# Routing softmax moved behind the FFN's router, FFN weights split once and loaded as halves

## The reference, cut to what matters

```python
# FFN (second stage): 1376 hidden columns, padded to 11 chunks of 128
scores = sigmoid(x @ W_router)                    # 8 low-rank experts, top 2
gate = x @ W_gate + lora(x, sA_gate, sB_gate) + expert_lora(x, A_gate, B_gate, w)
up   = x @ W_up   + lora(x, sA_up, sB_up)     + expert_lora(x, A_up, B_up, w)
hidden = silu(gate) * up
out = hidden @ W_down + lora(hidden, ...) + expert_lora(hidden, ...)

# mixture (fourth stage): routing over 64 experts
scores = softmax(xf @ router_w.T)
topk_w, topk_idx = top_k(scores, 8)
topk_w = topk_w / (topk_w.sum(-1) + 1e-20)
pos = (cumsum(onehot) * onehot).sum(-1) - 1       # place of a token in its expert's list
```

## Time and profile before

| | |
|---|---|
| median of 3 runs | 1468.19 us (1467.01 to 1469.37) |
| the profiled execution's own time | 1467.43 us |
| its span, first to last instruction | 1465.6 us |
| mean granted TensorE clock | 0.925 |
| PE busy | 1249.2 us, 85% |
| VectorE, ScalarE, GpSimd busy | 750.8, 508.1, 521.9 us |
| moved by DMA | 181.07 MB |

### The profile page before, as it was taken

How to read it: one execution, slowest core, us unless ns; L and a number is a source line. 1 busy time by engine, 2 the same in 40 slices (tenths; PEclk the granted TensorE clock), 3 DMA queues, 4 the chain that set the end, 5 groups by cost and what they waited for, 6 DMA issues and landing times. The chain is left out here.

```text
span 1465.6 us, 19315 instructions
## 1 busy us (share of the span) xinstructions
PE 1249.2 (85%) x6516; PEld 911.3 (62%) x6516; DVE 750.8 (51%) x1441; ACT 508.1 (35%) x1145; POOL 521.9 (36%) x539
## 2 busy tenths in 40 slices
PE   0698999887899988789998778999637999999990
PEld 0566777655777765577776557777435666666660
DVE  7674645576666667666666766452571222222220
ACT  1582322565232156523215652221122323333330
POOL 3530323633033373302337330132104455555551
PEclk9998999997989999888999988899857999999995
DMA  7002221000322100032210002541415999999966
GB/s 256 1 1 89 79 105 53 0 1 30 121 92 92 53 1 1 30 121 98 85 53 1 2 30 85 204 172 67 194 61 168 334 333 343 358 353 351 292 103 129
DMA packets 45600, 181.07 MB, mean 124 GB/s; under 512 B 6412, under 2 KB 9484, under 8 KB 36692
## 3 DMA queue, kind: packets, MB, share of 16 engines
q1 hardware_dynamic: 30660, 140.23, 25.5%
q0 software_dynamic: 14864, 39.85, 12.0%
HBM read 149.36 MB, written 34.90 MB: 126 GB/s over the span
## 5 line engine op out<-in xcount | busy, mean ns | idle before, releaser
L2024 PE MATMUL PS<-WE,XGT 128*128 128x384 f32 x512 | 195.1, 504 | 1.5 <-DVE HM L1597 0.8
L678 POOL CAST HH<-HID 128x512 fp32r<-128x512 f32 x44 | 38.9, 884 | 366.5 <-DVE HID L1504 366.5
L810 ACT ACTIVATE P<-PS,NM 128x512 f32<-128x512 f32 (+3 forms) x256 | 132.3, 539 | 51.4 <-DVE NM L1217 50.6
L1620 PE MATMUL PS<-XTH,WHI 128*128 128x512 f32 x352 | 144.2, 410 | 0.3 <-ACT SIL L953 0.3
L1621 PE MATMUL PS<-XTL,WHI 128*128 128x512 f32 x352 | 141.0, 401 | 0.0
L1622 PE MATMUL PS<-XTH,WLO 128*128 128x512 f32 x352 | 140.5, 399 | 0.0
L1457 DVE TENSOR_TENSOR WLO<-WRAW,WHI 128x584 fp32r<-128x584 f32 (+1 forms) x88 | 109.7, 1246 | 38.6 <-ACT WHI L939 30.8
L2024 PEld LDWEIGHTS PS<-WE,XGT 128*128 128x128 f32 x512 | 88.2, 192 | 57.9 <-issue 23.5
L1217 DVE TENSOR_REDUCE NM<-PS 128x2 f32<-128x1024 f32 (+2 forms) x96 | 98.6, 1041 | 49.7 <-PE PS L1629 49.2
L1680 PE MATMUL PS<-ident,P 128*128 128x128 f32 x640 | 105.2, 305 | 21.9 <-ACT P L810 12.7
L939 ACT ACTIVATE WHI<-WRAW 128x1280 fp32r<-128x1280 f32 x44 | 56.1, 1274 | 167.4 <-DMA WRAW<-in_ffn 161.6
(11 more groups left out here) (282 smaller groups left out, 2811.3 us busy)
## 6 DMA issues: line engine op xcount, KB each, us to landing
WE<-in_we SPq DMA_DIRECT2D x64, 1152.0 KB, 8.1
WRAW<-in_ffn SPq DMA_DIRECT2D x44, 932.0 KB, 4.6
acc<-HN SPq DMA_DIRECT2D x17, 256.0 KB, 5.1
XIN<-in_x SPq DMA_DIRECT2D x4, 1024.0 KB, 9.4
out<-X SPq DMA_DIRECT2D x4, 1024.0 KB, 4.2
out<-acc POOLq DMA_DIRECT2D x1, 4096.0 KB, 23.3
hx<-HN SPq DMA_DIRECT2D x3, 1152.0 KB, 4.8
CTX<-in_ctx SPq DMA_DIRECT2D x4, 256.0 KB, 6.7
```

The costliest lines, as they stand in the source:

```text
L810: act.activation(prob(t, n), PS[:, c0:c0 + (t + 1) * P], ACT.Exp, bias=NM[:, c:c + 1], accum_out=SSUM[:, c:c + 1]).then_inc(S["p_ready"], 1)
L1620: pe.matmul(dst, a[0], b_[0], start=first, stop=False, **kw)
L2024: mm = pe.matmul(bank(2 + s % 2, 0, 2 * F1), XGT[s % 2][:, k, :], WE[s][:, k * 2 * F1:(k + 1) * 2 * F1], start=(k == 0), stop=(k == KC - 1))
```

## The change

Three things change.

1. The routing softmax of batch b-1 is cut in two. `gates_begin` (row maximum, subtraction) stays ahead of the router's chain; `gates_rest` moves behind chunk 0. With it front_norms of the next batch moves from behind chunk 0 to behind chunk 1, front_scales from chunk 1 to chunk 2, PE's `positions` from chunk 0 to chunk 1, VectorE's from chunk 1 to chunk 3. The one-hot matmuls of the lists come in two pairs (at chunks 4 and 8) in place of single tiles at 2, 4, 6, 8; their first matmul now opens the bank, and the two zeroing matmuls per batch go.
2. The weights are split in batch 0 only. WHI and WLO are replaced by WGU (high and rest of the gate and up piece, 128 x 2560) and WDN (of the down piece, 128 x 1168), two slots each. Batch 0 stores each to a new DRAM tensor `split`, 1280 KB and 584 KB a chunk.
3. Batches 1 to 3 load both back, 1280 KB and 584 KB a chunk, straight into WGU and WDN, with semaphores of their own. The load of WGU waits until gate_up(f-2) is done on PE, that of WDN until down(f-2) is done. WRAW, ScalarE's copies and VectorE's subtractions are not used there.

```diff
-    WHI = [sb(f"WHI{s}", [P, WCOLS], F32R) for s in range(2)]
-    WLO = [sb(f"WLO{s}", [P, WCOLS], F32R) for s in range(2)]
+    WGU = [sb(f"WGU{s}", [P, 2, WD], F32R) for s in range(2)]
+    WDN = [sb(f"WDN{s}", [P, 2, WCOLS - WD], F32R) for s in range(2)]
...
+            def store_gu(f):
+                sp.wait_ge(S["wg_hi"], 1 + f + 1)
+                sp.wait_ge(S["wg_lo"], 1 + f + 1)
+                alone(sp, "sp")
+                sp.dma_start(split[span(f, P), 0:2 * WD], flat(WGU[f % 2])).then_inc(split_stored[f % 2], 16)
...
+                if b == 0:
+                    sp.dma_start(WRAW[0][:, :], w["ffn"][0:P, :]).then_inc(w_loaded[0], 16)
+                    sp.dma_start(WRAW[1][:, :], w["ffn"][P:2 * P, :]).then_inc(w_loaded[1], 16)
+                else:
+                    for slot in range(2):
+                        sp.wait_ge(split_stored[slot], 32 * SLOT_LOADS[slot])
+                    for f in range(2):
+                        load_gu(f)
+                        load_dn(f)
...
                 if b > 0:
                     store_rows(b - 1)
...
+                if b == 0:
+                    store_gu(0)
                 for f in range(2, NF):
-                    load_w(f, f % 2)
+                    if b == 0:
+                        store_gu(f - 1)
+                        down_made(f - 2)
+                        sp.dma_start(WRAW[f % 2][:, :], w["ffn"][span(f, P), :]).then_inc(w_loaded[f % 2], 16)
+                        store_dn(f - 2)
+                    else:
+                        sp.wait_ge(S["up_ps"], 1 + b * NF + f - 1)
+                        alone(sp, "sp")
+                        load_gu(f)
+                        sp.wait_ge(S["dn_ps"], 1 + b * NF + f - 1)
+                        alone(sp, "sp")
+                        load_dn(f)
                     if last and f < 8:
                         load_expert(f - 2, f - 2)
...
+                def wg_hi(f, slot):
+
+                    act.wait_ge(w_loaded[slot], 16 * (f // 2 + 1))
+                    if f > 1:
+                        act.wait_ge(split_stored[slot], 32 * (f // 2))
+                    act.activation(WGU[slot][:, 0, :], WRAW[slot][:, 0:WD], ACT.Copy).then_inc(S["wg_hi"], 1)
...
-                w_rest(0, 0, 0, WD, "wg_hi", "wg_lo")
-                if b > 0:
+                if b == 0:
+                    w_rest(0, WGU, 0, WD, "wg_hi", "wg_lo")
+                else:
                     dve.wait_ge(S["lgt_ps"], 1 + b)
-                    gates(b - 1, bank(1, 0, NT * E1).rearrange("p (t e) -> p t e", t=NT))
+                    gates_begin(b - 1, bank(1, 0, NT * E1).rearrange("p (t e) -> p t e", t=NT))
...
                 chunk(0, 0)
-                if not last:
-                    front_norms(b + 1)
+                if b > 0:
+                    gates_rest(b - 1)
...
-                        if d == 1 and i == 0 and not last:
-                            front_scales(b + 1)
+                        if i == 0 and not last:
+                            (front_norms if d == 1 else front_scales)(b + 1)
...
                 def gate_up(f, slot, parts="weights lora"):
-                    hi, lo = WHI[slot], WLO[slot]
-                    pe.wait_ge(S["wg_lo"], 1 + b * NF + f + 1)
+                    hi, lo = WGU[slot][:, 0, :], WGU[slot][:, 1, :]
+                    if b == 0:
+                        pe.wait_ge(S["wg_lo"], 1 + f + 1)
+                    else:
+                        pe.wait_ge(gu_loaded[slot], 16 * ((b - 1) * SLOT_LOADS[slot] + f // 2 + 1))
```

More of the change, by code:

```diff
@@ L84, in end, with build @@
         assert self.n == self.per, (self.sem, self.n, self.per)
[L87 removed]
+def build(nc, x, ctx_in, w, out, hx, acc, split):
     place = {"at": 16896}
@@ L323, in build @@
     w_loaded = [sem("w_loaded0"), sem("w_loaded1")]
+    split_stored = [sem(f"split_stored{s}") for s in range(2)]
+    gu_loaded, dn_loaded = ([sem(f"{part}_loaded{s}") for s in range(2)] for part in ("gu", "dn"))
+    SLOT_LOADS = (NF // 2 + 1, NF // 2)
     M = {n: sem("m_" + n) for n in ("idx xgt_ps xgt_sb gu_ps sil wc hm_twice hm hmt_ps hmt_sb y_ps y_sb added".split())}
@@ L508, in load_expert, with flat, load_gu, load_dn @@
                 sp.dma_start(WE[s][:, :], w["we"][span(e, P), :]).then_inc(expert_loaded[s], 16)
+            def flat(tile):
+                return tile[:, :, :].rearrange("p h c -> p (h c)").bitcast(F32)
+            def load_gu(f):
+                sp.dma_start(flat(WGU[f % 2]), split[span(f, P), 0:2 * WD]).then_inc(gu_loaded[f % 2], 16)
+            def load_dn(f):
+                sp.dma_start(flat(WDN[f % 2]), split[span(f, P), 2 * WD:2 * WCOLS]).then_inc(dn_loaded[f % 2], 16)
+            def store_gu(f):
[3 more added lines that the diff above has]
+                sp.dma_start(split[span(f, P), 0:2 * WD], flat(WGU[f % 2])).then_inc(split_stored[f % 2], 16)
+            def down_made(f):
+                sp.wait_ge(S["wd_hi"], 1 + f + 1)
+                sp.wait_ge(S["wd_lo"], 1 + f + 1)
+                alone(sp, "sp")
+            def store_dn(f):
+                sp.dma_start(split[span(f, P), 2 * WD:2 * WCOLS], flat(WDN[f % 2])).then_inc(split_stored[f % 2], 16)
             def feed(b):
@@ L945, in ffn, with wd_hi @@
                 act.activation(r8[0][:, :, :], projected[:, :, 0:E0], ACT.Exp, scale=-1.0).then_inc(S["sig_ready"], 1)
-                def wd_hi(slot):
-                    act.activation(WHI[slot][:, WD:WCOLS], WRAW[slot][:, WD:WCOLS], ACT.Copy).then_inc(S["wd_hi"], 1)
+                def wd_hi(f, slot):
+                    if f > 1:
+                        act.wait_ge(split_stored[slot], 32 * (f // 2))
+                    act.activation(WDN[slot][:, 0, :], WRAW[slot][:, WD:WCOLS], ACT.Copy).then_inc(S["wd_hi"], 1)
                 def silu(f):
@@ L968, in ffn @@
                 act.activation(WXT[:, :], bank(3, parts=LR), ACT.Copy).then_inc(S["wxT_sb"], 1)
[L969 to L974 removed]
+                for f in range(NF):
+                    chunk(f, f % 2)
+                if b == 0:
+                    for slot in range(2):
+                        act.wait_ge(split_stored[slot], 32 * SLOT_LOADS[slot])
                 act.wait_ge(S["ld_ready"], 1 + b + 1)
@@ L1493, in ffn, with chunk @@
                     "lg_ready", b + 1)
-                def chunk(f, slot, last=False, meanwhile=lambda: None):
-                    if not last:
-                        w_rest(f + 1, 1 - slot, 0, WD, "wg_hi", "wg_lo")
-                    w_rest(f, slot, WD, WCOLS, "wd_hi", "wd_lo")
-                    meanwhile()
+                def chunk(f, slot, last=False):
+                    if b == 0:
+                        if not last:
+                            w_rest(f + 1, WGU, 0, WD, "wg_hi", "wg_lo")
+                        w_rest(f, WDN, WD, WCOLS, "wd_hi", "wd_lo")
                     dve.wait_ge(S["sil_ready"], 1 + b * NF + f + 1)
@@ L1841, in positions, with one_hots @@
                 mm.then_inc(S["pos_ps"], 1)
-            def one_hots(bk, high, low, last):
+            def one_hots(bk, high, low, first, last):
                 for e in range(0, E1, GE):
                     mm = pe.matmul(bank(bk, e * SB, (e + GE) * SB), high[:, e:e + GE, :].rearrange("p e a -> p (e a)"),
-                                   low[:, e:e + GE, :].rearrange("p e c -> p (e c)"), start=False, stop=last,
+                                   low[:, e:e + GE, :].rearrange("p e c -> p (e c)"),
+                                   start=(first and e == 0), stop=last,
                                    skip_group_check=True)
                 return mm
-            def clear(bk):
-                pe.matmul(bank(bk), zrow[:, 0:P], zrow[:, :], start=True, stop=False, skip_group_check=True)
             def list_step(b, f):
-                if f == 0:
+                if f == 1:
                     pe.wait_ge(lists_loaded, 16 * len(LISTS))
```

133 lines of the change are left out of this document (63 added, 70 removed).

## The result

The changed kernel takes 1481.82 us (median of 4 runs, 1477.72 to 1486.54) against 1467.98 (1467.01 to 1469.37) for the kernel before: ratio 1.0100, 95% interval 1.0072 to 1.0128. On another chip it took 1477.5 (5 runs) against 1465.23: 1.0086, 1.0068 to 1.0104. It is about 0.9% slower. The forecast was 1460, faster, with a range of 1449 to 1475; all of that is too low. The profiled execution took 1477.72 us, of which 1475.9 are the span; before, the span was 1465.6. So 10.3 us have to be found.

What follows compares the result with a forecast made beforehand. PE, busy for 85% of the span, was taken to bound the kernel. The terms 22.2 + 1.5 - 7.0 - 8.5 = 8.2 us gained took 1467.43 to 1459.2, median 1460, with an eight-in-ten range of 1449 to 1475.

Steps and rivals of the forecast that it cites:

- the term for the stores in batch 0: Batch 0's FFN: copies waiting on queued stores and loads make a ring of 11.6 us a turn; loss 8.5 us.
- Rival 1: Batch 0's ring: alternating loads and stores run at 334 to 358 GB/s, loss 19 to 23 us, 1472.5; chance 0.2.
- the shared count: Batch 0: ScalarE's copy for chunk f waits until WRAW(f) is loaded and both stores of chunk f-2 have landed.
- The turn of 12.8: Batch 0's ring at the skill's 358 GB/s: 2.86 million bytes take 8.0 us, loss 19 us.
- the gain at the starts and the zeroing matmuls: Batches 1 to 3, from G (first weight matmul of gate_up(0)) to gate_up(2): 22.2 us gained; six zeroing matmuls gone, 1.5 us.
- the stall ahead of gate_up(2): Batches 1 to 3: WGU's load lands late behind the store to hx; waits 4.4 us plus slow clock 2.6, 7.0 together.
- the steady chunks: Steady part of the FFN, batches 1 to 3: removing the splitting buys nothing; PE's chunks stay as before.
- The 0.9 us of room in batch 3's chunks: Batch 3: loads with an expert's 1152 KB between them take 9.5 us, inside one chunk by 0.9 us.
- the third (stores hide): Batch 0's ring turns below 10.5 us, the stalls stay; 16.7 us gained, 1451.5; chance 0.2.
- the fourth: Start of batches 1 to 3: PE still idles at LG, the 22.2 us are gone, only costs stay, 1475; chance 0.03.
- The second's sum: Batches 1 to 3: store to hx stalls 3 us each with slow clock, ring as forecast; 1.2 us gained, 1467; chance 0.15.
- The list of what would show it: Signs in the profile after; wrong if batch 0's HIDs exceed 12.5 us apart, gate_up(2) waits over 3, or batch 3 waits.

Runs made afterwards that it cites:

- e8_stores_alone: Changed kernel, with batch 0's WRAW loads for chunks 2 to 10 replaced by stores of the same size to a spare tensor; 1464.76 us, ratio 0.9979.
- e1_counts: Changed kernel, with batch 0's two halves of a chunk counting their stores on separate semaphores; 1464.76 us, ratio 0.9988 to the kernel before.
- e2_load_first: e1_counts, with WRAW's load for chunk f also issued ahead of the store of WGU(f-1); 1454.53 us, ratio 0.9926 to the kernel before.
- e9_order_only: Changed kernel, with WRAW's load issued ahead of the store of WGU(f-1), both halves still on one semaphore; 1489.98 us, ratio 1.0172.
- e3_hx_later: Changed kernel, with the store of HN to hx issued behind the load of WGU for chunk 2; 1468.12 us, ratio 1.0018.
- e6_both_mended: e2_load_first, with the store to hx behind the load of WGU for chunk 2; 1441.78 us, ratio 0.9831 to the kernel before.
- e5_softmax_hx_later: Kernel before with only the softmax's part of the change, and the store to hx behind WRAW's load for chunk 2; 1442.51 us, ratio 0.9820.
- e7_split_only: Changed kernel, with the softmax's rest called ahead of the FFN's router as in the kernel before; 1481.8 us, ratio 1.0098.

## Why the prediction was wrong, step by step

**The step that failed: the term for the stores in batch 0, 8.5 us (bounds 0 to 23).** It measured 26.4 to 26.6. The direction was right, a ring that turns slower than PE; its size was off by a factor of three, and even the upper bound was passed. The turn was to be 11.6 and was 13.55. From 155.0, where the first turn starts, to gate_up(10) are nine turns, so 2 us a turn make the 18.6 us that the loss of 7.8 lacked. They fall in two parts:

- *The rate, 13.9 us.* The step added 4.7 us for stores at 407 GB/s and 2.2 for loads at 438, stretches with one direction only. For one direction the same arithmetic nearly holds: with stores alone (e8_stores_alone) the turn was 11.99 where it gives 11.8. With both directions the rate is 333 to 346. At 339 the step's own arithmetic gives 8.4 + 1.8 + 3.0 = 13.2, and the six short turns took 13.1 on average. Rival 1 had this rate, 334 to 358, from the page's busiest slices; its turn of 12.8 to 13.3 was the nearest of all. I gave it 0.2 because indirect transfers lie in those slices too. Slices in which both directions mix were the nearest rows to the new work, and stretches of one direction were not.
- *Three long turns, 4.7 us.* Each of them holds a packet of the instruction queue, and in them the copy starts 10.3 to 10.5 us behind the issue of WDN's store, where it is 8.9 to 9.3 in the others. No term of the step stood for this. That the packet delays the store is not shown; no run took it away.

Since the first turn, too, was long (14.6), there was no slack: gate_up(2) waited 1.41 us, where 1.5 us in hand were forecast.

**What the step had right and did not question: the shared count.** It let the copy wait for "both stores of chunk f-2", so this is inside its 11.6 and is no part of the miss. But it is a cause of the slow kernel, shown by taking it away: with a count for each half the turn falls to 12.08 at the same mixed rate (e1_counts). Order and count together bring it to 10.38, where PE sets the pace (e2_load_first). The order alone makes it worse (e9_order_only). So these two edits are not additive: from 13.62 the one gives -1.5, the other +1.1, both -3.2.

The Trainium skill (DMA: Bandwidth & Descriptors, section Specifications) gives a core's share of HBM as about 358 GB/s. The mixed stretches agree with it within 7%, at 333 to 346; the stores alone, at 414, do not. No run here shows that this share is what sets the mixed rate. The turn of 12.8 that the prediction worked out from it was nearer than mine.

**Right: the gain at the starts and the zeroing matmuls, 22.2 + 1.5 = 23.7.** Without the stall G to gate_up(2) is 23.3 us in batches 1 to 3 (e3_hx_later, e6_both_mended), as forecast. With the two faults mended, G to HID(10) is shorter by 8.0, 8.3 and 6.9 us in batches 1 to 3 (e6_both_mended against before), 23.2 together. In e5_softmax_hx_later, without any of the split, it is 8.0, 8.3 and 8.4, 24.7. So the softmax's half alone gives the whole gain; e7_split_only shows that the split alone would give some of the same us.

**Mechanism right, size small: the stall ahead of gate_up(2), 7.0 us (bounds 0 to 14).** gates_ready came at 431.74, G + 16.37, forecast G + 16.3. The load of WGU landed about 9.4 us after its issue (432.32 to 441.77), where 8.0 were forecast; waits of 2.98, 1.89 and 3.49 are 8.4, where 4.4 were, and by e3_hx_later the whole term was 10.0, 0.7 of them waits for weights in batch 3. The mis-sized part is again the rate: the stretch of this landing shows 323 GB/s at a DMA share of 0.94, 344 while at work, and 2.49 million bytes at 344 with the fixed 2.0 give 9.2.

**Right: the steady chunks.** HID(2) to HID(10) takes 85.34 us in batches 1 and 2, before 85.66; the splitting that went was hidden. The 0.9 us of room in batch 3's chunks was not enough: two waits there of 0.6 us, ahead of gate_up(6) and (8), inside the bound of 7.

**The sum, corrected.** 23.7 - 10.0 - 26.6 = -12.9; measured in the span -10.3, and the median of the first set -13.8. Of the other rivals, the third (stores hide) is what e2_load_first made of the kernel, not what the change did; the fourth is refuted, LG waits no more. The second's sum needed the ring as forecast.

The list of what would show it called this right: HIDs over 12.5 apart in batch 0, a wait over 3 us at gate_up(2) (3.49 in batch 3), waits for weights in batch 3.

**Open.** Whether the instruction packets make the three long turns, or only come with them, was not tried. With the ordering of e2_load_first the same packets are there and no wait is. Nor is it settled what spreads the runs of one kernel, 9 and 18 us in the two sets of the changed kernel, 2 in one set of the kernel before and 13 in a longer one: a lower granted clock ahead of the FFN goes with 4.8 us of one run, but nothing shows what brought it on. In the twelve profiles G of batch 0, where the changed lines have hardly had a part yet, lies between 141.9 and 149.9 us; differences of a few us between single profiles' totals say little.

## What to carry to other kernels

Where transfers of both directions will be in flight, take the rate from a stretch in which both are, and follow every waiting instruction to the last transfer that its count covers: a count shared by two transfers costs as much as the slower rate did here. A load that is needed next goes ahead of stores that nobody waits for, and a store whose data come late is not put into a queue ahead of a load that could go at once. Before work is taken off an engine with half its time free, ask for the path: here the whole gain of 1.7% came without the split, from moving 5 us of softmax by one chunk (with the small steps that move along and two zeroing matmuls fewer a batch) and one store by one place, and splitting the weights once added nothing measurable to it.
